# A hand-ordered attention and MLP layer on one NeuronCore: grouping four MLP units, moving transposed scores, one gate and one projection

## The reference, cut to what matters

```python
x  = L0_attn_query                              # (4, 256, 256): 4 batches of 256 tokens, 256 features
xn = layernorm(x)
# attention: 16 heads of 16, softmax over 256 keys, in each batch
mixed = xn @ Wqkv.T                             # q, k, v
s = softmax(q @ k.T / 4) @ v                    # per head
s = s @ Wproj.T + bproj
# MLP
h = gelu(xn @ proj1.T + proj1_bias)             # 1024 hidden
g = silu(h @ proj2.T + proj2_bias)
out = x + s * g
```

## Time and profile before

| | |
|---|---|
| time, median of 3 runs | 118.74 us (118.61 to 119.44) |
| profiled execution | 119.02 us |
| its span, first to last instruction | 117.1 us |
| PE busy | 111.1 us (95%) |
| DVE busy | 86.7 us (74%) |
| ACT busy | 76.3 us (65%) |
| POOL busy | 71.4 us (61%) |

### The profile page before, as it was taken

The page is one execution under the profiler, slowest core; times in us unless marked ns, Lnnn a source line. Parts: engine busy times, 40 slices in busy tenths (PEclk is TensorE's granted clock), DMA queues, the critical chain, the costliest instruction groups (busy, mean ns, idle before and its releaser), DMA issues.

```text
span 117.1 us, 2969 instructions
## 1 busy us (share of the span) xinstructions
PE 111.1 (95%) x1114; PEld 89.2 (76%) x1114; DVE 86.7 (74%) x158; ACT 76.3 (65%) x112; POOL 71.4 (61%) x92
## 2 busy tenths in 40 slices
PE   5989999999999999999999999999999999899980
PEld 5579998868888998889788888875866848476660
DVE  0689994444979988987498898053977868999761
ACT  5064696476676830385977887979968698789100
POOL 4227579029998640097948866999690763816470
PEclk9999999999999999999999999999999999999998
DMA  3999946466523564663000003700000000020213
GB/s 92 348 340 377 316 144 209 139 203 208 202 55 91 172 208 145 193 211 106 1 7 8 0 0 55 306 6 4 7 7 10 0 0 6 0 90 6 90 62 120
DMA packets 9634, 13.30 MB, mean 114 GB/s; under 512 B 2452, under 2 KB 4884, under 8 KB 9492
## 3 DMA queue, kind: packets, MB, share of 16 engines
q1 hardware_dynamic: 9060, 12.82, 33.6%
q10 hardware_dynamic: 560, 0.30, 0.9%
HBM read 5.51 MB, written 1.05 MB: 56 GB/s over the span
## 4 chain that ended last, share of the span: by engine, by line
PE 44%; SPq 29%; issue 7%; DVE 6%; DMA 5%; POOL 4%; ACT 2%; DVEq 0%; POOLq 0%
SPq L407 28%; PE bank L958 10%; PE bank L1018 9%; PE bank L847 7%; PE bank L1001 5%; PE bank L985 4%; DMA ks<-stage 3%; PE bank L971 3%; PE bank L998 2%; DMA xs<-x 2%; PE bank L1029 1%; POOL bg L518 1%; POOL xb L520 1%; PE bank L881 1%; SPq L396 1%
## 5 line engine op out<-in xcount | busy, mean ns | idle before, releaser
L738 DVE TENSOR_REDUCE negm<-bank 128x4 f32<-128x1024 f32 x32 | 37.8, 1219 | 8.4 <-PE bank L971 8.1
L499 POOL TENSOR_TENSOR hTl<-hG,hTh 128x512 fp32r<-128x512 f32 x16 | 20.3, 1295 | 6.0 <-ACT hTh L612 6.0
L623 ACT ACTIVATE PT<-bank 128x1024 f32<-128x1024 f32 x16 | 15.7, 1025 | 4.0 <-PE bank L985 4.0
L608 ACT ACTIVATE hG<-bank,b1s 128x512 f32<-128x512 f32 x16 | 10.9, 679 | 6.7 <-PE bank L958 6.7
L971 PEld LDWEIGHTS bank<-ks,qs 48*128 48x128 f32 x128 | 11.4, 186 | 2.6 <-DMA ks<-stage 0.5
L971 PE MATMUL bank<-ks,qs 48*128 48x256 f32 x128 | 13.0, 281 | 0.2 <-DMA ks<-stage 0.2
L958 PE MATMUL bank<-w2s,hTh 64*128 64x512 f32 x64 | 12.1, 399 | 0.0
L1001 PE MATMUL bank<-w2s,hTh 128*128 128x512 f32 x32 | 11.9, 410 | 0.0
L958 PE MATMUL bank<-xTh,w1h 64*128 64x512 f32 x64 | 11.0, 422 | 0.1
L985 PEld LDWEIGHTS bank<-qs,ks 50*128 50x128 f32 x128 | 8.4, 186 | 3.4 <-issue 1.6
L958 PE MATMUL bank<-xTh,w1l 64*128 64x512 f32 x64 | 10.9, 391 | 0.0
(11 more groups left out here) (108 smaller groups left out, 255.4 us busy)
## 6 DMA issues: line engine op xcount, KB each, us to landing
qs<-stage SPq DMA_DIRECT2D x24, 128.0 KB, 2.9
ks<-stage SPq DMA_DIRECT2D x24, 128.0 KB, 2.9
xs<-x SPq DMA_DIRECT2D x4, 256.0 KB, 3.9
w_raw<-w SPq DMA_DIRECT2D x1, 1024.0 KB, 7.7
w_in_place<-w SPq DMA_DIRECT2D x1, 1024.0 KB, 10.4
xb<-x SPq DMA_DIRECT2D x1, 1024.0 KB, 5.4
wqkv_raw<-wqkv SPq DMA_DIRECT2D x3, 256.0 KB, 4.6
out<-fin SPq DMA_DIRECT2D x6, 128.0 KB, 1.9
```

What stands on the lines that cost most here:

```text
L499: nc.gpsimd.tensor_tensor(hTl[:, n % FC, :], hG[:, n % FC, :], hTh[:, n % FC, :].bitcast(f32), ALU.subtract).then_inc(h_lo, 1)
L608: nc.scalar.activation(hG[:, f, :], bank_of(*s), ACT.Gelu, bias=b1s[:, f:f + 1]).then_inc(gelu_done, 1)
L623: nc.scalar.activation(exp_of(w), scores_of(*s), ACT.Exp).then_inc(exp_done, 1)
L738: nc.vector.tensor_reduce(negm[:, j, :, s[1] % 2, b, :], scores_of(*s), axis=AX.X, op=ALU.max, negate=True).then_inc(max_done, 1)
```

## The change

Four edits, all in the order of steps and what follows from it.

1. `S_PLAN`, `pieces` and `BEHIND` become `PLAN` and `turns`. Units 0 to 3 are one group with the turns (0,1), (2,3), (1,0), (3,2): a unit's second turn comes two turns behind its first. Its four scores stand behind pieces 3, 4, 6 and 7 (they stood behind piece 3 of the first pair, and 1, 2 and 3 of the second). On ACT the high part of the hidden units becomes a step `H` of its own; in this group GELU 0, GELU 1 and the copy of unit 0 come when six pieces are made, and GELU 2, GELU 3 and the copies of 1, 2 and 3 after the eighth. All other pairs keep their order.
2. `MID_ST`: `ST 0`, `ST 1` and `ST 2` (with `TANH 0` and `TANH 1`) stand behind pieces 1, 3 and 5 of the last `R2` pair, where they stood behind 2, 4 and 6.
3. `GATE 7` on DVE moves from ahead of `PJ 0` to behind `PV 9` and `FIN 1`; `FIN 0` and `FIN 1` move behind DVE's part of `PV 9`; `BIAS 7` moves behind `PV 11`, which on POOL is still ahead of `TURN 0 2`.
4. The end: `PJ 6` is finished ahead of the first half of `PJ 7`.

```diff
-BEHIND = {("RV", 0): [("MROWS",)], ("R1", 5): [("TANH", 2), ("TANH", 3)]}
-MID_ST = {2: [("ST", 0), ("TANH", 0)], 4: [("ST", 1), ("TANH", 1)], 6: [("ST", 2)]}
-S_PLAN = [("R1", 0, (3,)), ("R1", 1, (1, 2, 3)), ("R1", 2, (1, 3)), ("R1", 3, (1, 2, 3)), ("RV", 0, (1, 3)),
-          ("R2", 0, (0, 2, 3, 5, 6)), ("R2", 1, (0, 1, 3, 5, 7)), ("R1", 4, (1, 2, 3)), ("R1", 5, (1, 3)),
-          ("R1", 6, (1, 2, 3)), ("R1", 7, (1, 2, 3))]
+TURNS = {2: ((0, 1), (1, 0)), 4: ((0, 1), (2, 3), (1, 0), (3, 2))}
+PLAN = [("R1", (0, 1, 2, 3), (3, 4, 6, 7)), ("R1", (4, 5), (1, 3)), ("R1", (6, 7), (1, 2, 3)), ("RV", (0, 1), (1, 3)),
+        ("R2", (0, 1), (0, 2, 3, 5, 6)), ("R2", (2, 3), (0, 1, 3, 5, 7)),
+        ("R1", (8, 9), (1, 2, 3)), ("R1", (10, 11), (1, 3)), ("R1", (12, 13), (1, 2, 3)), ("R1", (14, 15), (1, 2, 3))]
+MID_ST = {1: [("ST", 0), ("TANH", 0)], 3: [("ST", 1), ("TANH", 1)], 5: [("ST", 2)]}
...
+            if len(group) == 4 and n == 5:
+                order += [("F1", group[0]), ("F1", group[1]), ("H", group[0])]
+        if len(group) == 4:
+            order += [("F1", group[2]), ("F1", group[3])] + [("H", u) for u in group[1:]]
+        elif kind == "R1":
+            for u in group:
+                order += [("F1", u), ("H", u)]
...
-    order += st(7) + [("TURN", 1, 1), ("GATE", 7)] + bias(6, 7) + pj(0, 1) + fin(0, 1) + pv(9) + st(8) + pv(10, 11)
+    order += st(7) + [("TURN", 1, 1)] + bias(6) + pj(0, 1) + pv(9) + fin(0, 1) + [("GATE", 7)] + st(8) + pv(10, 11) + bias(7)
...
-    return order + pj(5) + [("PJ", 6, 0), ("PJ", 7, 0), ("FIN", 5), ("PJ", 6, 1), ("FIN", 6), ("PJ", 7, 1), ("FIN", 7)]
+    return order + pj(5) + [("PJ", 6, 0), ("FIN", 5), ("PJ", 6, 1), ("FIN", 6)] + pj(7) + fin(7)
...
-                    act.wait_ge(gelu_done, n_f1)
+                elif s[0] == "H":
+                    f = s[1] % FC
+                    act.wait_ge(gelu_done, s[1] + 1)
                     nc.scalar.activation(hTh[:, f, :], hG[:, f, :], ACT.Copy).then_inc(h_hi, 1)
...
-                    if (turn, part) == (0, 0):
-                        for one in both:
-                            wait_free(one)
-                    if (turn, part) == (1, 0):
-                        n_turn += 2
-                        pe.wait_ge(turn_made, n_turn)
+                    begins = turn < len(turns(p)) // 2
+                    if part == 0:
+                        if begins:
+                            for one in both:
+                                wait_free(one)
+                        else:
+                            n_turn += 2
+                            pe.wait_ge(turn_made, n_turn)
```

More of the change, by code:

```diff
@@ L57, in members, with turns @@
     if kind == "RV":
[L58 to L64, removed]
+        return [("V", 1, n) for n in PLAN[p][1]]
+    return [({"R1": "F1", "R2": "F2"}[kind], n) + (part if kind == "R2" else ()) for n in PLAN[p][1]]
+def turns(p):
+    return TURNS[len(PLAN[p][1])]
 def build_order():
@@ L86, in build_order @@
     units = [("S", w) for w in range(2 * GROUPS)]
-    for kind, p, behind in S_PLAN:
-        for n, piece in enumerate(pieces(kind, p)):
+    for p, (kind, group, behind) in enumerate(PLAN):
+        pieces = [(kind, p, turn, part) for turn in range(len(turns(p))) for part in range(PARTS[kind])]
+        for n, piece in enumerate(pieces):
             order.append(piece)
-            if n in behind:
+            for _ in range(behind.count(n)):
                 order.append(units.pop(0))
-            if (kind, p) == ("R2", 1):
+            if (kind, group) == ("R2", (2, 3)):
                 order += MID_ST.get(n, [])
-        order += members(kind, p, 3) + BEHIND.get((kind, p), [])
+            if len(group) == 4 and n == 5:
[6 more added lines that the diff above has]
+        else:
+            order += members(kind, p, 3)
+        if group[-1] >= 11 and ("TANH", 2) not in order:
+            order += [("TANH", 2), ("TANH", 3)]
+        if kind == "RV":
+            order.append(("MROWS",))
     assert not units
@@ L297, in banks @@
                 elif s[0] in PARTS:
-                    if s[2:] == (0, 0):
-                        for one in members(*s[:2], 0):
-                            place(n, one)
+                    if s[3] == 0:
+                        both = [members(*s[:2], 0)[k] for k in turns(s[1])[s[2]]]
+                        for one in both:
+                            if one not in home:
+                                place(n, one)
                 elif s[0] in ("XT", "QK", "S", "ST", "PV", "PJ") or s[:2] == ("V", 0) or s[:2] in SPOTS:
@@ L906, in _ @@
                     kind, p, turn, part = s
-                    both = members(kind, p, 0)
-                    if (turn, part) == (0, 0):
-                        for one in both:
-                            wait_free(one)
-                    if (turn, part) == (1, 0):
-                        n_turn += 2
-                        pe.wait_ge(turn_made, n_turn)
-                    first, end = (turn, part) == (0, 0), part == PARTS[kind] - 1
+                    group = members(kind, p, 0)
+                    both = [group[k] for k in turns(p)[turn]]
+                    begins = turn < len(turns(p)) // 2
+                    if part == 0:
+                        if begins:
+                            for one in both:
+                                wait_free(one)
+                        else:
+                            n_turn += 2
+                            pe.wait_ge(turn_made, n_turn)
+                    first, end = begins and part == 0, part == PARTS[kind] - 1
                     if kind == "R1":
@@ L928, in _ @@
                     else:
-                        pe.wait_ge(h_lo, FC * (p // 2) + 2 * part + 2)
+                        pe.wait_ge(h_lo, FC * (both[0][1] // EARLY) + 2 * part + 2)
                         pe.wait_ge(w2_lo, 2)
@@ L936, in _ @@
                         for half in range(2):
-                            one = both[turn ^ half]
+                            one = both[half]
                             rows = slice(64 * half, 64 * half + 64)
@@ L957, in _ @@
                             done = end and n == len(todo) - 1
-                            m = nc.tensor.matmul(dst, lhs, rhs, start=first and n == 0, stop=done and turn == 1)
+                            m = nc.tensor.matmul(dst, lhs, rhs, start=first and n == 0, stop=done and not begins)
                             if done:
-                                m.then_inc(made if turn == 1 else turn_made, 1)
+                                m.then_inc(turn_made if begins else made, 1)
                 elif s[0] == "S":
```

## The result

The changed kernel took 117.42 us in the median of four runs (117.27 to 117.66) against 118.71 (118.61 to 119.44), ratio 0.9876, 95% interval 0.9827 to 0.9925. The forecast was 118.2, with 117.6 as its lower end: the direction was right, the size too small. The same kernel was timed twice more beside its parts, with ratios 0.9900 (0.9836 to 0.9964) and 0.9935 (0.9903 to 0.9967). The three intervals share 0.9903 to 0.9925, so a gain of 0.9 to 1.15 us agrees with all three, and the 1.29 us of the first measurement is the largest of the three.

What follows compares the result with a forecast made beforehand. The stacking DMAs' landing at `S 20` was taken to bound the first half, then PE's own work with a bend at `PV 10`. Profiled 119.02 + 0 + 0 - 0.5 + 0 = 118.5, or 118.2 against the median; range 117.6 to 119.0.

Steps and rivals of the forecast that it cites:

- edit 4's term: At the end, tile 6's store issued 0.44 us sooner leaves queues freer for the last: 0 to 0.1, taken as 0.
- value at the end 0: Edit 1's 0.3 us saved on PE is hidden at `S 20`; edit 2's cost and gain are also put at 0.
- a clock that runs beside PE: At `S 20`: the last stacking DMA lands at 56.16, so PE savings between 24 and 56 us are waited away.
- PE waited for none of them before `S 20`: Edit 2 brings ACT's exponentials earlier, but PE did not wait for them before `S 20`: gain zero.
- PE was free at 56.03: Slack at `S 20`: PE free at 56.03, data at 56.16, start at 56.20 after 0.17 us idle.
- both gains count: Rival at `S 20`: the landing comes earlier with PE, so edit 1's gain stays too: 117.8; chance 0.15.
- POOL's end: POOL ends its eighth low part at 42.0, the same moment as before, so the maxima it splits next start unchanged.
- I take 50.2: Landing of ACT's eight DMAs for the maxima, needed by `ST 0`: 50.2, about mid-bounds 49.8 to 50.7, cost 0.
- the outer bound of 50.95: Latest landing of the maxima's DMAs, since `ST 0` did not idle before; landing then would cost 0.55 us.
- The rival of a slower kernel: GELU 0 slips, POOL and the maxima's landing come late, PE reaches `S 20` 1.0 us late: 119.25; chance 0.12.
- late next: Behind `PV 10` in the tail: ACT's exponentials follow 0.56 sooner, then DVE limits, with a gain of 0.3 taken.
- The third rival: In the tail, port sharing with POOL makes DVE 0.5 later, shrinking the gain to 0.1: 118.65; chance 0.2.

Runs made afterwards that it cites:

- the landing out of the way: Edit 1 alone on the kernel before, with the two DMAs of ones issued by ACT before GELU 6 and before the values: 118.77 us, ratio 1.0007.
- the copy: The kernel before, unchanged, profiled a second time: 118.68 us, ratio 0.9996.

## Why the prediction was wrong

Two terms that the sum put at nothing were worth something: edit 4, and edits 1 and 2 together.

The step that failed by most, on average over the landings, is **edit 4's term**. "0 to 0.1. I take 0" measured 0.32. PE and DVE behaved as argued, and the queues were named as the place of a gain; its size was guessed where the trace of before had it. There the stores of tiles 6 and 7, issued 0.10 us apart, took 1.9 and 2.0 us to land, while tile 5's, 1.3 us ahead of them, took 1.7:

```profile
out<-fin SPq DMA_DIRECT2D x1, 128.0 KB, 1.7
```

**Edits 1 and 2, "value at the end 0" each.** Near enough for each alone by the traces (edit 1: `S 21` 0.10 later with the landing out of the way; edit 2: the end 0.11 sooner), wrong for the pair, which is worth up to 0.44 and 0.19 on average. The sentence that failed is that `S 20` is "a clock that runs beside PE". It is two clocks, and one of them, `ST 2`'s exponential, is what edit 2 moves, while edit 1 gives PE back the time that the earlier `ST 0` would wait. So it takes both; "PE waited for none of them before `S 20`" was true and beside the point, since PE waits for it one step behind. The other, the landing, was read from one execution, and moves by 3 us between executions. The slack was misread too: "PE was free at 56.03" is the end of a matmul, but `S 20` starts 0.23 us behind the start of PE's last R2 matmul where nothing is waited for (the copy), and 0.56 behind it in the profile of before, so 0.33 us were waited there. The rival "both gains count" named a sum (117.8) near the one that the parts make, for a wrong reason: the landing did not come earlier with PE.

**Edit 1 on PE.** Expected 0.3 saved with a wait of 0.2 in the second turn. The wait was 0.27 and the bubble is gone: `S 0` comes 0.24 sooner, and `S 4` 0.42. Then the `b2s` halving, which the prediction does not mention at all, took it back. I had worked out POOL's end (42.0; it came at 32.10 + 8.95 = 41.05 in an execution whose R1 started 0.59 sooner, so 41.64 on the scale of before), but not what else on DVE would fall into POOL's unbroken run.

**Edit 2's wait.** "I take 50.2" for the landing of the maxima was too early. Without edit 1, `ST 0` was released at 50.80 and at 50.56 on the scale of before (edit 2 alone; edits 2, 3 and 4), 3.3 and 3.0 us behind the last issue, where the prediction's bounds were 2.0 and 2.9; only the outer bound of 50.95 held. `ST 0` then waits 0.43 and 0.19 us. With edit 1, which issues those DMAs 0.4 us sooner, it does not wait, so the term of 0 came true by edit 1 and not as argued. The rival of a slower kernel did not come. One reading was off and did no harm: the two evacuations start at 48.79 in the earlier trace rows, so the banks are free at 49.9 and not 49.6.

**Edit 3.** The mechanism was right, -0.56 at `PV 10` (0.64 measured) and -0.5 at the end (0.41). What was "late next" was named wrongly. ACT "had been idle there, so they follow" overlooks that the idle time was one gap of 0.53 us behind `ST 26`'s exponential, and that `ST 29` needs the bank which that exponential frees. DVE did gain by port sharing as argued, and more than the 0.3 taken. `FIN 0`, `FIN 1` and `GATE 7` of the changed kernel, and the scalings behind them, in DVE's timeline:

```profile
101.33 0.72 DVE L844 TENSOR_TENSOR fin<-fin,xb 128x256 f32<-128x256 f32 x2
101.97 0.42 DVE L710 SCALAR_TENSOR_TENSOR gate<-th,yh 128x256 f32<-128x256 f32 x1
...
103.56 1.02 DVE L796 TENSOR_TENSOR ctxn<-cd,rc 128x128 f32<-128x128 f32 x2
```

With POOL idle, the two `FIN` take 0.72 for 1.38 and the gate 0.42 for 0.95, so 1.2 us are gained; the scalings beside `BIAS 7` take 1.02 for 0.49 and give 0.5 back. The third rival stays away.

**The number.** Edit 3 (0.41), edit 4 (0.32) and the pair (0.19) put the sum at 117.8 against 118.71, a ratio of 0.9922, which the two later measurements bear out. The rest of the way to 117.42 is the first sample of four, which was a lucky one. An estimate from the traces: R1 at 23.4, `S 21` 33.69 behind it with an early landing, 58.45 to the end and 1.8 around the span make 117.3 for the changed kernel, and 23.4, 34.10, 59.18 and 1.8 make 118.5 for the one before. Three of the first four executions lay at 117.27 to 117.43, at that floor; of the eighteen later ones only 117.34 and 117.38 did.

## What to carry to other kernels

A wait that ends exactly when another would have ended hides it: before calling a place "held by X", take X away on paper and look for the next instruction that waits there, one step further on as well. A landing read from one execution is a sample; price an edit ahead of it over several. And when an edit closes the gaps of an engine that shares a port, list every operation of the other engine that falls into the closed stretch, the small forgotten ones first.

## What the runs showed of the hardware

- A DVE `TENSOR_SCALAR` with one SBUF input took 1.26 us instead of 0.28 inside POOL's run of subtractions. I had counted on two inputs only. The Trainium skill (SBUF — State Buffer, Who interferes with whom) lists `tensor_scalar` among the operations that can take the ports shared with GpSimd in a 2-port mode, and says that the loser blocks for the whole instruction. The 0.98 us more, less than POOL's 1.28 for one low part, agree with that; which mode the operation ran in, no run here shows.
- Two DMAs of 64 KB that fill four partitions with ones cost 3 to 5 us of a queue wherever they stood in these runs. SP's own issues behind them at the start, kernel before with the ones moved:

```profile
3.79 1.78 SPq L379 DMA_DIRECT2D wqkv_raw<-wqkv  x1
5.61 1.76 SPq L380 DMA_DIRECT2D w_raw<-w  x1
7.41 1.48 SPq L381 DMA_DIRECT2D w_in_place<-w  x1
```

  These took 0.43, 0.43 and 0.69 us before. The ones were issued by ACT, so DMAs on one engine's queue held up issues on the other's.
- PE's first four transposes took 1.08 us in the profile of before and 0.67 in the unchanged copy, and everything behind was 0.45 us later. First line: before; second: the copy.

```profile
6.19 1.08 PE L881 MATMUL bank<-ident,xs 128*128 128x128 f32 x4 [0.38 <-DVE xs L674]
```

```profile
6.16 0.67 PE L881 MATMUL bank<-ident,xs 128*128 128x128 f32 x4 [0.34 <-DVE xs L674]
```

  The page shows a granted clock of 1.00 there in both, but the trace's clock records begin only at 7.14 us in the profile of before and at 6.05 in the copy; ahead of the first record the page's 1.00 stands for no record. The transposes follow that moment. With a first record at 4.39 to 6.27 us they took 0.67 or 0.68 us (14 traces), at 6.60 it was 0.83, at 6.83 it was 0.95, and at 7.14 to 7.29 it was 1.07 or 1.08 (3 traces); the one trace without records took 1.09. With SP's queue as before, R1 began at 23.38 to 23.69 us in the fast ones and at 23.96 to 24.02 in the slow ones. So most of the head start of the changed kernel's profile goes with its first record coming sooner (4.98 us), in steps that both kernels share. That the clock was at its lower level until then is argued from the pace (0.42 us for one transpose, 0.27 behind the record). What makes it rise sooner or later, behind the same ten matmuls on PE, stays open.
